# A graph network of four layers on one core: sender rows picked by VectorE instead of a mask product, and a ring of eight groups for the second layer's gathered rows

## The reference

```python
h = relu(layernorm(x)); x = x + lightgcn(h, 3 hops)            # first layer
h = relu(layernorm(x)); x = x + relu(gcn(h, edge_weight, W, b)) # second: sum over edges of h[src] * norm
h = relu(layernorm(x)); x = x + h @ W_self.T + mean(h[src]) @ W_neigh.T   # third
h = relu(layernorm(x))                                          # fourth: message network
m = relu(relu(concat(h[src], h[dst], edge_attr) @ W1 + b1) @ W2 + b2)
agg = segment_sum(m, dst)
y = relu(concat(h, agg) @ nW1 + nb1) @ nW2 + nb2
x = x + h + layernorm(y) * scale + offset
```

## Time and profile before

| | us |
|---|---|
| median of three runs | 1410.26 |
| lowest and highest | 1403.56, 1423.4 |
| the profiled execution | 1414.13 |
| its span in the trace | 1412.1 |
| TensorE busy in it | 1130.3 |
| VectorE busy in it | 852.6 |
| GpSimd busy in it | 601.7 |

### The profile page before, as it was taken

The page is one execution under the profiler, slowest core; times in us unless marked ns, Lnnn a source line. Parts: engine busy times, 40 slices in busy tenths (PEclk is TensorE's granted clock), DMA queues, the critical chain, the costliest instruction groups (busy, mean ns, idle before and its releaser), DMA issues.

```text
span 1412.1 us, 27295 instructions
## 1 busy us (share of the span) xinstructions
PE 1130.3 (80%) x7006; PEld 765.0 (54%) x7006; DVE 852.6 (60%) x2837; ACT 385.5 (27%) x827; POOL 601.7 (43%) x769
## 2 busy tenths in 40 slices
PE   4889879996978777888596888878788787878786
PEld 2556545544745555557264555655565565556554
DVE  8999985468756464564667444454454545445455
ACT  3677751113212121211033222222222222222221
POOL 5434410004566656662004655544555454455540
PEclk8999989998989988898696998988989898988897
DMA  2000031001011111112305444433443344444431
GB/s 50 1 0 0 0 154 52 0 1 36 17 21 22 20 20 20 20 20 90 124 15 157 118 101 93 105 85 94 92 92 98 93 103 89 92 97 96 99 87 31
DMA packets 142550, 88.46 MB, mean 63 GB/s; under 512 B 98717, under 2 KB 120794, under 8 KB 142378
## 3 DMA queue, kind: packets, MB, share of 16 engines
q1 hardware_dynamic: 124168, 70.31, 18.8%
q0 software_dynamic: 16960, 17.40, 6.8%
q10 hardware_dynamic: 1378, 0.22, 0.1%
HBM read 75.51 MB, written 12.35 MB: 62 GB/s over the span
## 4 chain that ended last, share of the span: by engine, by line
PE 56%; DVE 15%; issue 12%; another core or an unknown queue 11%; ACT 3%; DVEq 3%; ACTq 1%; DMA 0%; SPq 0%
PE seg L1502 10%; PE big L1532 7%; PE seg L1543 7%; PE seg L1617 5%; PE big L1653 5%; PE big L1430 4%; PE seg L1661 4%; PE seg L1671 3%; PE big L1643 3%; ACT A L1242 2%; PE seg L1553 2%; DVE acc_mem L1902 2%; PE seg L1613 1%; PE big L1654 1%
## 5 line engine op out<-in xcount | busy, mean ns | idle before, releaser
L1130 POOL DMA_INDIRECT A<-table,idx x338 | 323.3, 957 | 308.8 <-ACT idx L1218 194.1
L1130 POOL DMA_INDIRECT pair<-table,idx x192 | 191.5, 997 | 263.0 <-issue 195.9
L1365 ACT COPY A<-big 128x512 f32<-128x512 f32 x104 | 60.8, 584 | 361.1 <-remote 237.4
L1430 PE MATMUL big<-acc_mem 128*128 128x500 f16 x416 | 123.9, 413 | 26.8 <-DVE acc_mem L1902 12.1
L1671 PE MATMUL seg<-A 128*64 128x42 f32 x832 | 76.0, 247 | 83.3 <-DVE acc_mem L1742 77.1
L1661 PEld LDWEIGHTS seg<-A 128*128 128x128 f32 x832 | 116.7, 202 | 47.3 <-issue 42.7
L1543 PE MATMUL seg<-A,cur 128*64 128x160 f32 x700 | 118.2, 314 | 28.9 <-issue 26.6
L1242 ACT CAST A<-big 128x500 f32 x208 | 125.4, 603 | 49.2 <-PE big L1433 26.0
L1298 ACT COPY A<-big 128x500 f32<-128x500 f32 x112 | 62.5, 579 | 251.9 <-remote 125.2
L1532 PE MATMUL big<-A 128*128 128x500 bf16 x448 | 123.0, 420 | 8.1 <-issue 6.4
L1502 PE MATMUL seg<-A,acc_mem 128*128 128x512 f16 (+1 forms) x525 | 109.2, 365 | 24.4 <-DVEq L2030 16.5
(11 more groups left out here) (255 smaller groups left out, 1637.5 us busy)
## 6 DMA issues: line engine op xcount, KB each, us to landing
A<-drel_flat SPq DMA_DIRECT2D x104, 252.0 KB
A<-in_edge_attr_dram SPq DMA_DIRECT2D x103, 128.0 KB
spilled_adjacency<-A SPq DMA_DIRECT2D x1, 7074.0 KB, 18.3
A<-spilled_adjacency SPq DMA_DIRECT2D x6, 1152.0 KB, 12.9
A<-table,idx POOLq DMA_INDIRECT x338
A<-in_src_dram SPq DMA_DIRECT2D x78, 64.0 KB
A<-pr_table SPq DMA_DIRECT2D x104, 31.5 KB
pair<-table,idx POOLq DMA_INDIRECT x192
```

Of the source, the lines that this page charges most:

```text
L1130: pool.indirect_dma_start(out=rows[:, q, j, 0:D], out_offset=None, in_=table, in_offset=bass.IndirectOffsetOnAxis(ap=idx[:, q, j:j + 1], a ...
L1430: nc.tensor.matmul(big[:, k % 4, 0:PC], hot_l[:, h, :, (2 * k + j) % 8], hot_r[:, 2 * (k % 4) + j, :], start=(j == 0), stop=(j == 1))
```

## The change

Two changes are joined.

The ring: `rows1` and `idx` get an index u, the round's parity, so the ring holds eight groups. The landings of odd rounds count on semaphores of their own (`gathered_odd`). The gathers of the first two rounds wait for no sum; those of round `it` wait for the sum of round it - 2, and so does the copy of their indices. In the second layer and in the fourth `gathers_begun` is raised for each gather and not for each group.

The made rows: the product with `others` goes, and with it the splitting of keys in `senders`. The low nine bits of the sources are computed once in the preparation, turned to 16 bit by ScalarE and stored in `low_flat`; the keys are loaded from there, half as wide. The chunk of each edge's sender is computed once (`src_high`). `choose_rows` compares it with the numbers 0 to 6 (`chunk_of`), multiplies the seven candidates with the result (`picked`, in SBUF), and sums over the seven. The receivers (`drel_flat`, `drel_bc`) are stored and loaded in 16 bit too.

```diff
-        rows1 = pair[:, 0:Q * G * D].rearrange("p (q j d) -> p q j d", q=Q, j=G)
+        rows1 = pair[:, 0:2 * Q * G * D].rearrange("p (u q j d) -> p u q j d", u=2, q=Q, j=G)
...
+            def gather(row, index, done):
+
+                pool.sem_inc(gathers_begun, 1)
+                pool.indirect_dma_start(out=row, out_offset=None, in_=table,
+                                        in_offset=bass.IndirectOffsetOnAxis(ap=index, axis=0)).then_inc(done, 16)
+
+            def gather_round1(it, u):
+                for q in range(Q):
+                    pool.wait_ge(idx_ready[q], it + 1)
+                    if not (isinstance(it, int) and it < 2):
+                        pool.wait_ge(seg_done[q], it)
+                    for j in range(G):
+                        gather(rows1[:, u, q, j, :], idx[:, u, q, j:j + 1], (gathered, gathered_odd)[u][q])
...
-            def rows_summed(it, q):
-                pool.wait_ge(seg_done[q], 1 + it)
...
-            def next_idx1(it, q):
-                act.wait_ge(seg_done[q], 1 + it)
-                copy_idx(it, q)
+            def next_idx1(it, q, u):
+                act.wait_ge(seg_done[q], it)
+                copy_idx(it, q, u)
...
-            def idx_behind(b, q):
+            def idx_behind(b, u, q):
                 if q:
-                    if not (isinstance(b, int) and (b < 2 or b - 1 >= IT1)):
-                        next_idx1(b - 1, q - 1)
-                elif not (isinstance(b, int) and b < 3):
-                    next_idx1(b - 2, Q - 1)
+                    if not (isinstance(b, int) and (b < 2 or b >= IT1)):
+                        next_idx1(b, q - 1, u)
+                elif not (isinstance(b, int) and (b < 3 or b - 1 >= IT1)):
+                    next_idx1(b - 1, Q - 1, 1 - u)
...
-            def group_sums(it, q):
-                pe.wait_ge(gathered[q], (it + 1) * (16 * G))
+            def group_sums(it, turn, u, q):
+                pe.wait_ge((gathered, gathered_odd)[u][q], turn * (16 * G))
...
-                nc.tensor.matmul(made, hot_high[:, u, :], others, start=True, stop=False)
-                for m in (1, 2, 3, 0):
+                for m in range(4):
...
-                dve.tensor_scalar(keys_low[:, u, :], keys[:, u, :], SPAN - 1, None, ALU.bitwise_and).then_inc(ev("keys_split"), 1)
-                dve.tensor_scalar(keys_high[0:HIGH, u, :], keys[0:HIGH, u, :], 9, None, ALU.logical_shift_right).then_inc(ev("keys_split"), 1)
-                dve.wait_ge(ev("keys_split"), it * (2 * NM) + (2 * u + 2))
                 dve.wait_ge(rows_made, it * NM + (u + 1))
                 for m in range(4):
-                    dve.tensor_scalar(hot_low[:, u, m, :], keys_low[:, u, :], iota_4[:, m:m + 1], 1.0 / SCALE, ALU.is_equal, ALU.mult)
-                dve.tensor_scalar(hot_high[:, u, :], keys_high[0:HIGH, u, :], iota_p[0:HIGH, 0:1], None, ALU.is_equal).then_inc(senders_ready, 1)
+                    op = dve.tensor_scalar(hot_low[:, u, m, :], keys[:, u, :], iota_4[:, m:m + 1], 1.0 / SCALE, ALU.is_equal, ALU.mult)
+                op.then_inc(senders_ready, 1)
...
-                dve.wait_ge(rows_made, it * NM + (u + NM + 1))
+                m = it * NM + u
+                t = it * (Q * G) + (q * G + 2)
+                dve.tensor_scalar(chunk_of[:, u, :], iota_r[:, 0:HIGH], src_high[:, bass.ds(t, 1)], None, ALU.is_equal).then_inc(ev("chunk_found"), 1)
+                dve.wait_ge(ev("chunk_found"), m + 1)
+                dve.wait_ge(rows_made, m + (NM + 1))
+                dve.tensor_tensor(picked, made.rearrange("p (s f) -> p s f", f=D),
+                                  chunk_of[:, u, :].rearrange("p (s a) -> p s a", a=1).broadcast_to([P, HIGH, D]), ALU.mult).then_inc(ev("picked"), 1)
+                dve.wait_ge(ev("picked"), m + 1)
                 dve.wait_ge(transposed[q % 2], 1 + 2 * it + q // 2)
-                op = dve.tensor_reduce(X[:, q, 2, 0:D], made.rearrange("p (s f) -> p f s", f=D), AX.X, ALU.max)
+                op = dve.tensor_reduce(X[:, q, 2, 0:D], picked.rearrange("p s f -> p f s"), AX.X, ALU.add)
...
+            dve.tensor_scalar(src_low, raw_src, SPAN - 1, None, ALU.bitwise_and).then_inc(ev("src_parts_ready"), 1)
...
+            link(dve.tensor_scalar(src_high.bitcast(I32), src_i[:, 0:T], 9, None, ALU.logical_shift_right))
+            link(dve.tensor_copy(src_high, src_high.bitcast(I32)))
```

More of the change, by code:

```diff
@@ L747, in dense_path @@
         drel_t, src_t, dst_t, key_r_t, key_l_t, key_b_t, key_rest = (carve("prep", 4 * P) for _ in range(7))
+        src_low = carve("prep", 4 * P).bitcast(I32)
+        drel_16, low_16 = (carve("prep", 2 * P).bitcast(F16) for _ in range(2))
         below = carve("prep", 4 * THR)
@@ L898, in dense_path @@
         gathered = [sem(f"gathered{q}") for q in range(Q)]
+        gathered_odd = [sem(f"gathered_odd{q}") for q in range(Q)]
         idx_ready = [sem(f"idx_ready{q}") for q in range(Q)]
@@ L1032, in load_keys @@
                 sp.wait_ge(senders_ready, m + 1)
-                sp.dma_start(keys[:, u, :], src[bass.ds(tile * P, P)].partition_broadcast(P)).then_inc(keys_loaded[u], 16)
+                sp.dma_start(keys[:, u, :], low_flat[bass.ds(tile * P, P)].partition_broadcast(P)).then_inc(keys_loaded[u], 16)
             def keys_ahead(it, q):
@@ L1117, in pool_link, with gathers1, gathers3 @@
                 pool.wait_ge(pool_chain, pool_links[0])
-            def gathers(g, rows, slot_free):
-                pool.wait_ge(table_stored, 32 * (g + 1))
-                with pool.Fori(0, (IT1, IT)[g]) as it:
+            def gather(row, index, done):
[9 more added lines that the diff above has]
+                        gather(rows1[:, u, q, j, :], idx[:, u, q, j:j + 1], (gathered, gathered_odd)[u][q])
+            def gathers1():
+                pool.wait_ge(table_stored, 32)
+                for it in range(2):
+                    gather_round1(it, it)
+                with pool.Fori(1, IT1 // 2) as ii:
+                    for u in range(2):
+                        gather_round1(ii * 2 + u, u)
+            def gathers3():
+                pool.wait_ge(table_stored, 64)
+                with pool.Fori(0, IT) as it:
                     for q in range(Q):
-                        pool.wait_ge(idx_ready[q], g * IT1 + it + 1)
-                        slot_free(it, q)
-                        pool.sem_inc(gathers_begun, 1)
+                        pool.wait_ge(idx_ready[q], it + (IT1 + 1))
+                        rows_transposed(it, q)
                         for j in range(G):
[L1128 to L1132, removed]
-            def rows_summed(it, q):
-                pool.wait_ge(seg_done[q], 1 + it)
+                            if not (q in MADE and j == 2):
+                                gather(X[:, q, j, 0:D], idx[:, 0, q, j:j + 1], gathered[q])
             def rows_transposed(it, q):
@@ L1187, in on_gpsimd @@
             pool.iota(iota_4, [[P, 4]], base=0, channel_multiplier=1, allow_small_or_imprecise_dtypes=True).then_inc(ev("chooser_ready"), 1)
[L1188 to L1192, removed]
+            pool.wait_ge(ev("x_cleared"), 1)
+            gathers3()
         def steps(eng, stages, between=lambda s: None):
@@ L1281, in on_scalar @@
             act.wait_ge(ev("src_kept"), 1)
-            for q in range(Q):
-                copy_idx(0, q)
+            for it in range(2):
+                for q in range(Q):
+                    copy_idx(it, q, it)
             for k in range(ROUNDS):
@@ L1617, in make_rows @@
                         op = nc.tensor.matmul(made[:, 0:held.shape[2] * D], hot_low[:, u, m, :], held[:, k, :, :],
[L1618 removed]
+                                              start=(m == 0 and k == 0), stop=(m == 3 and k == 1))
                 if nodes_done(it, q, 1):
```

66 lines of the change are left out of this document (35 added, 31 removed).

## The result

The changed kernel is slower: the ratio to the kernel before is 1.032, 95% interval 1.017 to 1.048 (medians 1462.8 and 1416.8 us). In a second comparison, in another group of runs, it is 1.018 (1.012 to 1.024; 1474.2 and 1447.6). Chips and hours differ by as much as the change: the kernel before has medians from 1417 to 1448 us in five groups of runs (one chip gave 1447.6 in one group and 1420.8 in another), and 1184 us in one group, on a chip of its own. So every ratio here compares runs of one group on one chip.

The account below looks back on a forecast made before the run. TensorE's own work was taken as the first bound of the second and fourth layers, with most idle time in stretches beside gather runs. The terms, 0.4 + 0.5 - 15 + 15.6 = +1.5 us, gave 1412 us, range 1376 to 1440.

Parts of the forecast that it names:

- The opening of the ring: Second layer's start: 32 unbroken gathers instead of 16 may slow TensorE; taken as +5 us, between 0 and 16.
- Given back by the last sum: Second layer's end: the last round has no gathers beside it, which gives back 4.5 us, up to 8.5.
- The steady rounds: Second layer: gathers start when they start now, only for one round later; 0 us, rounds of 24 to 26 us.
- rival A: Second layer: GpSimd issues without stopping, a round takes 20 us and not 24.9; 54 us less, 1356; chance 0.08.
- rival D: Second layer: the ring does nothing since no wait it relaxes binds; part of the forecast, no chance of its own.
- The warning that holds move with the gathers: Forecast is wrong if stretches of single TensorE matmuls beside gather runs move with the gathers' new place; no size given.
- TensorE's saving: Fourth layer: 78 dropped mask matmuls at 0.29 us are 22.6 us, of which 15 were taken, 7.5 at the least.
- The choice: Fourth layer, third made group: VectorE's product, wait and reduce delay the transposes 0.6 us, 26 times, +15.6; bounds 0 and +29.
- The strided reduce: Fourth layer, choice of made rows: the reduce from SBUF, 256 bytes between neighbours, takes 0.62 us, as from PSUM.
- rival C: Fourth layer: strided reduce takes 1.24 us on the path, plus 16 for a slowed opening; 35 more, 1445; chance 0.15.
- Rival B: Fourth layer: choice is covered, all 22.6 us count, window-add waits shrink by 15; 42 us less, 1368; chance 0.17.
- Preparation: Before the layers: one more VectorE operation on the path, 0.43 us, and two ScalarE conversions; +0.4, at most +1.6.

## Why the prediction was wrong

It said 1412 us, no change, and slower by over 2% with a chance of 0.14. Going through its steps:

- **The opening of the ring** was taken at +5, between 0 and 16, nearer 0 because the first 16 gathers hold nothing. The first sum is 21 to 26 us later. The step that failed was to take 16 unheld gathers as a sign for the next 16. Even the bound of 16 was too low: it fits the idle time, 13 to 16 us more in 355 to 379 in three pairs of traces, and leaves out the granted clock, 0.54 to 0.63 in that stretch and 0.50 to 0.61 in the 6.5 us behind it. Given back by the last sum: forecast 4.5, measured 5, 12 and 14 in three pairs, two of them above its bound of 8.5. The ring's sum is +10.6 (5 to 16) instead of +0.5.
- **The steady rounds**: rival A did not come about, and the ring brings no gain of its own, as rival D said; what is given back behind the opening goes with fewer runs of twelve, as the table shows. The warning that holds move with the gathers was right and had no number in the sum.
- **TensorE's saving** was taken at 15 of 22.6: 10 was measured (3 to 20), so this term is not shown to be wrong. That not all of it counts is right; where the rest goes, to idle time or to the lower granted clock, is not shown.
- **The choice** was taken at 0.6 us of delay, 26 times. The product was right (0.625), the reduce 0.31 too short, and two errors came on top: 0.23 us was subtracted as slack, which is a latency, and the comparison with its wait (from 1109.73 to 1110.09, 0.36 us) stood in line, as the bound had allowed. A late choice is 0.36 + 0.62 + 0.13 + 0.92 = 2.0 us instead of 0.62. The idle time ahead of the third transposes rose by 1.1 to 1.7 us in the table; 26 times that is 29 to 44. This term, +15.6 in the sum, is the second step that failed, and the larger one. Taken by itself, with 1.07 us more of choice, it measured 16 us (4 to 27), so not all of the idle time is a loss of the whole; the made rows' 16 to 29 in three groups of runs plus the 10 given back make 26 to 39 for the whole choice. What makes up the rest beside the 16, the lower granted clock or the comparison and its waits, stays open.
- **The strided reduce** takes 0.934 us against 0.620 along the tile, 1.5 times, where rival C took twice and the forecast nothing. The Trainium skill, Advanced Engine Details and Errata, SBUF Cachelines, states a penalty where each access goes to another line of 16 bytes. The traces agree with its direction. Rival C is the case that came nearest, at 31 + 16 - 7.5 - 4.5 = 35 for a measured 46 (24 to 67) and 25 (17 to 34) in the two comparisons. That its choice is 1.4 us longer, as measured, is in part luck: the comparison stood in line for what the reduce fell short of. Its chance of 0.15 was too low: two of its three terms had rows that spoke for them, the 0.23 us and the idle time that follows a long run.
- **Rival B** fell with the 0.23 us: the choice is not covered, and the waits for the window add stayed (71.0 and 62.1 us before, 53.4 to 59.4 with the made rows alone).
- **Preparation**: the opening starts 0.6 us later (334.18 for 333.60; 0.3 in the second comparison), forecast 0.4.
- **Two readings** were off without moving the sum. The choices of the other two made groups end 3.7 us or more ahead of their transposes in most iterations, but only 1.8 us ahead in some; and the range of 1376 to 1440 does not take in most of rival C, whose own time is 1445.

## What to carry to other kernels

A gap that is the same in every iteration, like 0.23 us between a result and its user, is a latency and no slack: count nothing of it against added work. How much of added work is paid is another question; here it was 16 us of 26 x 1.07 = 28, with an interval of 4 to 27. Before an engine that isn't the bound is given longer unbroken runs of work, look at what the bounding engine does beside the runs that there are, sorted by their length; deepening a ring makes the first run as long as the ring, here 32 gathers instead of 16. And a step that becomes two passes over an intermediate in SBUF costs the second pass, a wait between them, and a strided side of one of them, so price the whole chain from input to release and not the operation that is added.

## What the runs showed of the hardware

- In all groups of runs but one TensorE was held beside unbroken runs of indirect gathers, with 5 to 6 us idle for 12 gathers and 19 to 29 for 32 in the second layer; on one chip it was not at all, beside runs of 104, and the kernel before took 1184 us there instead of 1417 to 1448. During a hold matmuls start some 0.7 us or a multiple of it apart. The gathers' packets keep moving evenly, most of them 0.7 us behind the start of each issue, so no backlog of them shows, and only one packet of the queues that load instructions falls into 355 to 379. The cause was not found.
- A reduce on VectorE over 7 values for 64 features takes 0.620 us along an SBUF tile, 0.934 with 256 bytes between neighbours, and 0.625 with the same stride in PSUM (there a maximum and not a sum); a product of 448 words written to SBUF takes 0.625 straight and 0.966 with a stride of 28 bytes.
- With 18.5 us more idle time of TensorE its granted clock over the whole fourth layer was 0.81 instead of 0.85, and its busy time fell by 6.5 us where 74 dropped matmuls should have saved 21. That the idle time is what lowered the clock is not shown, but the lower clock is no chance of one trace: over the whole kernel it is 0.847 to 0.852 in four runs of the made rows alone and 0.863 to 0.872 in twelve of before on the same chip.
